# A Mamba and LSTM kernel: sigmoids made on ScalarE, and the LSTM's cell in plain VectorE operations

## The reference

```
def step(carry, xt):
    h, c = carry
    g = xt @ wih.T + h @ whh.T + bih + bhh
    i, f, gg, o = jnp.split(g, 4, axis=-1)
    c = jax.nn.sigmoid(f) * c + jax.nn.sigmoid(i) * jnp.tanh(gg)
    h = jax.nn.sigmoid(o) * jnp.tanh(c)
    return ((h, c), h)
...
comb = jnp.concatenate([m, lf, lb], axis=-1)
return comb @ fusion_w.T + fusion_b
```

## Time and profile before

| | |
|---|---|
| median of 3 runs | 2211.43 us (2204.95 to 2212.78) |
| span of the profiled execution, first to last instruction | 2159.5 us |
| median less that span | 51.9 us |
| VectorE busy in the span | 1645.7 us |
| ScalarE busy | 1298.3 us |
| GpSimd busy | 1011.2 us |
| TensorE busy | 1857.5 us |

### The profile page before, as it was taken

The page is one execution under the profiler, slowest core; times in us unless marked ns, Lnnn a source line. Parts: engine busy times, 40 slices in busy tenths (PEclk is TensorE's granted clock), DMA queues, the critical chain, the costliest instruction groups (busy, mean ns, idle before and its releaser), DMA issues. The chain is left out here.

```text
span 2159.5 us, 49411 instructions
## 1 busy us (share of the span) xinstructions
PE 1857.5 (86%) x19547; PEld 1357.8 (63%) x19547; DVE 1645.7 (76%) x2609; ACT 1298.3 (60%) x2660; POOL 1011.2 (47%) x775
## 2 busy tenths in 40 slices
PE   7888888889888867897878878889788699999999
PEld 4444444444443323444568877767676599999999
DVE  4999999999999996678465442346554589999897
ACT  5777777777776645114345444252456388888886
POOL 1777777777777773110017777300440033333333
PEclk9999999999999999899679999898899699999999
DMA  3544444444444442520038889501730411112000
GB/s 130 167 132 132 126 137 132 132 132 127 128 139 140 132 137 55 126 45 1 7 100 236 258 257 256 139 1 73 231 114 12 187 64 64 65 65 69 14 7 7
DMA packets 98037, 241.63 MB, mean 112 GB/s; under 512 B 15024, under 2 KB 48320, under 8 KB 95504
## 3 DMA queue, kind: packets, MB, share of 16 engines
q1 hardware_dynamic: 89120, 218.12, 32.7%
q0 software_dynamic: 7680, 15.74, 3.2%
q10 hardware_dynamic: 1008, 4.62, 0.6%
HBM read 226.25 MB, written 12.19 MB: 110 GB/s over the span
## 5 line engine op out<-in xcount | busy, mean ns | idle before, releaser
L1119 POOL TENSOR_TENSOR dBu<-du,Bs 128x858 f32<-128x858 f32 (+1 forms) x240 | 588.2, 2452 | 203.4 <-DVE hst L1046 94.6
L574 PE MATMUL py<-hst,ident 128*128 128x429 f32 (+1 forms) x960 | 416.7, 565 | 95.9 <-DVE hst L1056 95.1
L1046 DVE TENSOR_TENSOR_SCAN hst<-dA,dBu 128x858 f32<-128x858 f32 (+1 forms) x240 | 457.8, 1908 | 17.1 <-ACT dA L889 13.7
L889 ACT ACTIVATE dA<-dt,negA 128x416 f32<-128x416 f32 (+1 forms) x480 | 269.5, 596 | 177.2 <-DVE hst L1046 175.6
L574 PEld LDWEIGHTS py<-hst,ident 128*128 128x128 f32 x960 | 183.6, 202 | 292.3 <-DVE hst L1056 169.0
L3444 POOL TENSOR_TENSOR hm<-h,mw 128x264 f32<-128x264 f32 x128 | 89.7, 701 | 391.0 <-DVE h L3424 391.0
L1056 DVE TENSOR_TENSOR hst<-hst,Cs 128x858 f32<-128x858 f32 (+1 forms) x240 | 246.5, 1027 | 0.0
L3315 PE MATMUL pg<-hs,wh 128*128 128x66 f16 x6144 | 218.8, 194 | 4.8 <-issue 4.7
L3315 PE MATMUL pg<-xm,wi 128*128 128x66 f16 x6144 | 214.6, 195 | 6.8 <-issue 5.4
L3315 PEld LDWEIGHTS pg<-hs,wh 128*128 128x128 f16 x6144 | 204.8, 98 | 8.6 <-issue 5.1
L3315 PEld LDWEIGHTS pg<-xm,wi 128*128 128x128 f16 x6144 | 202.0, 98 | 11.3 <-issue 5.9
(11 more groups left out here) (568 smaller groups left out, 3458.8 us busy)
## 6 DMA issues: line engine op xcount, KB each, us to landing
wb<-sf_w SPq DMA_DIRECT2D x96, 514.0 KB, 4.9
Bs<-bc_rows SPq DMA_DIRECT2D x96, 429.0 KB, 4.6
Cs<-bc_rows SPq DMA_DIRECT2D x96, 429.0 KB, 3.5
mw<-route_weights SPq DMA_DIRECT2D x8, 2112.0 KB, 10.1
wb<-gf_w SPq DMA_DIRECT2D x24, 514.0 KB, 4.9
Bs<-bc_rows SPq DMA_DIRECT2D x24, 396.0 KB, 5.0
Cs<-bc_rows SPq DMA_DIRECT2D x24, 396.0 KB, 4.6
mb<-route_masks SPq DMA_DIRECT2D x8, 1088.0 KB, 5.8
```

Of the source, the lines that this page charges most:

```text
L574: return nc.tensor.matmul(out, weight, moving, **kw)
L889: last = a(o, by_seq(dt[:, j % 2, h, 0:n])[:, :, 1:S], ACT.Exp, scale=negA[:, l, h * DST + k:h * DST + k + 1])
L1046: v.tensor_tensor_scan(hst[:, g % HR, 0:2 * n], dA[:, g % 2, 0:2 * n], dBu[:, g % 2, 0:2 * n], 0.0, ALU.mult, ALU.add).then_inc(h_ready, 1)
L1119: g_.tensor_tensor(dBu[:, g % 2, 0:2 * n].rearrange("p (a n) -> p a n", a=2), du[:, j % 2, :, 0:n], Bs[:, q % NBS, k % BG, 0:n].unsqueeze( ...
```

## The change

Each step gets one more activation: after the four tanhs ScalarE turns the three tanhs of half gates into sigmoids in place, (x/2 + 1/2) over 3 x 64 columns, with the column of halves `half` that GpSimd sets once. It waits on `tanhed` for the third tanh. The cell is then the plain one. tanh(g) and the cell lie side by side in `gc`, so that both products are one multiply over 2 x 64 columns (`prod`), and an add makes the cell. h is one multiply. Nothing is doubled, and the two halvings of weights go.

```
-        cz = sb("cz", [128, 2, NB])
-        ig = sb("ig", [128, NB])
+        half = sb("half", [128, 1])
+        gc = sb("gc", [128, 2, NB])
+        prod = sb("prod", [128, 2, NB])
...
             def lstm(t):
                 if t == 0:
                     pe.wait_ge(l_loaded, 112)
-                    pe.wait_ge(lw_ready, 3)
                     pe.wait_ge(z_gated, 2)
...
                 for g in range(3):
-                    a(act3[:, g, :], pre[:, g, :], ACT.Tanh, scale=0.5, bias=lb[:, 2, g:g + 1])
-                a(cz[:, 0, :], pre[:, 3, :], ACT.Tanh, bias=lb[:, 0, 3:4]).then_inc(gated, 1)
+                    last = a(act3[:, g, :], pre[:, g, :], ACT.Tanh, scale=0.5, bias=lb[:, 2, g:g + 1])
+                last.then_inc(tanhed, 1)
+                a(gc[:, 0, :], pre[:, 3, :], ACT.Tanh, bias=lb[:, 0, 3:4])
+                act.wait_ge(tanhed, t + 1)
+                a(act3, act3, ACT.Identity, scale=0.5, bias=half[:, :]).then_inc(gated, 1)
 
             def lstm_cell(t):
                 act.wait_ge(c_ready, t + 1)
-                a(tc[:, :], cz[:, 1, :], ACT.Tanh, scale=0.5).then_inc(tc_ready, 1)
+                a(tc[:, :], gc[:, 1, :], ACT.Tanh).then_inc(tc_ready, 1)
...
-            a(whh[:, :, :, :], whh[:, :, :, :], ACT.Copy, scale=0.5).then_inc(lw_ready, 1)
-            a(fw[:, 1, :], fw[:, 1, :], ACT.Copy, scale=0.5).then_inc(lw_ready, 1)
...
             def lstm_c(t):
                 dve.wait_ge(gated, t + 1)
                 if t >= 1:
+                    dve.wait_ge(c_ready, t)
+                v.tensor_tensor(prod[:, :, :], act3[:, 0:2, :], gc[:, :, :], ALU.mult).then_inc(prods_ready, 1)
+                dve.wait_ge(prods_ready, t + 1)
+                if t >= 1:
                     dve.wait_ge(tc_ready, t)
-                    dve.wait_ge(c_ready, t)
-                v.scalar_tensor_tensor(out=ig[:, :], in0=act3[:, 0, :], scalar=1.0, in1=cz[:, 0, :],
-                                       op0=ALU.add, op1=ALU.mult).then_inc(prods_ready, 1)
-                v.scalar_tensor_tensor(out=act3[:, 1, :], in0=act3[:, 1, :], scalar=1.0, in1=cz[:, 1, :],
-                                       op0=ALU.add, op1=ALU.mult).then_inc(prods_ready, 1)
-                dve.wait_ge(prods_ready, 2 * t + 2)
-                v.scalar_tensor_tensor(out=cz[:, 1, :], in0=act3[:, 1, :], scalar=0.5, in1=ig[:, :],
-                                       op0=ALU.mult, op1=ALU.add).then_inc(c_ready, 1)
+                v.tensor_tensor(gc[:, 1, :], prod[:, 0, :], prod[:, 1, :], ALU.add).then_inc(c_ready, 1)
...
-                v.scalar_tensor_tensor(out=hr[:, t % 2, :], in0=act3[:, 2, :], scalar=1.0, in1=tc[:, :],
-                                       op0=ALU.add, op1=ALU.mult).then_inc(r_ready, 1)
+                v.tensor_tensor(hr[:, t % 2, :], act3[:, 2, :], tc[:, :], ALU.mult).then_inc(r_ready, 1)
```

More of the change, by code:

```diff
@@ L499, in mamba_lstm @@
             stage(nc, "wop_ready wop_kept cent_ready cent_kept sq_ready var_ready var_kept var_logged rstd_ready m_scaled m_done"))
-        (diag_ready, bias_set, lw_ready, gates_ready, gated, prods_ready, c_ready, tc_ready, r_ready, hs_kept, fused, fused_added) = ctx.enter_context(
-            stage(nc, "diag_ready bias_set lw_ready gates_ready gated prods_ready c_ready tc_ready r_ready hs_kept fused fused_added"))
+        (diag_ready, bias_set, lw_ready, gates_ready, half_set, tanhed, gated, prods_ready, c_ready, tc_ready, r_ready, hs_kept, fused, fused_added) = ctx.enter_context(
+            stage(nc, "diag_ready bias_set lw_ready gates_ready half_set tanhed gated prods_ready c_ready tc_ready r_ready hs_kept fused fused_added"))
         b_loaded = ctx.enter_context(stage(nc, " ".join(f"b_loaded{k}" for k in range(NBS))))
@@ L920, in _ @@
             decay(2)
-            act.wait_ge(lw_ready, 3)
+            act.wait_ge(lw_ready, 1)
+            act.wait_ge(half_set, 1)
             lstm_gates(0)
@@ L977, in _ @@
             v.memset(dA[:, :, :], 0.0).then_inc(dA_zeroed, 1)
-            v.memset(cz[:, 1, :], 0.0)
+            v.memset(gc[:, 1, :], 0.0)
             def soften(j):
@@ L1099, in _ @@
             g_.memset(edge[:, 1:2], 4000.0 / 32).then_inc(edge_set, 1)
+            g_.memset(half[:, :], 0.5).then_inc(half_set, 1)
             g_.memset(whh[:, :, :, :], 0.0).then_inc(l_zeroed, 1)
```

## The result

The changed kernel takes 2246.63 us (2244.49 to 2252.69, 5 runs) against 2211.43 (2204.95 to 2221.88) before: 1.0156 times, 95% interval 1.0135 to 1.0177. It is slower by some 35 us, where -0.15 had been forecast, and lies outside the range of 2204 to 2219.

A forecast was written before the change was run, and what follows sets the result against it. VectorE was taken to set the pace, except in ScalarE's chain to scan 8. Losses of 1.46 us from ScalarE's added work minus 1.61 us saved on VectorE gave -0.15 us, so 2211.3 us, range 2204 to 2219.

The forecast's parts named there:

- the cell on VectorE: LSTM cell's operations on VectorE: product to scan 0.465 us after the change, 0.07 less; add of 228 ns.
- The operation for h: VectorE's multiply that makes h in each LSTM step: would still take 0.13 us of VectorE.
- the saving of 0.07 us a step: VectorE's cell: 0.07 us less per step, arriving in 23 of the 33 steps, 1.61 us.
- ScalarE's activation: Added operation over 192 columns in PSUM: 378 ns long, ScalarE held 0.29 us longer per step.
- The 303 ns that the prediction set aside: Trainium skill's formula for the added 192-column ScalarE operation; with it the sum would be near -0.8 us.
- its delay is mostly swallowed: ScalarE's later gates: mostly absorbed by idle and existing waits, leaving 1.46 us of losses in all.
- Dropping the halvings: Two ScalarE activations before the scans go: worth 0, at most 0.9 us if dt were not the limit.
- B: Rival: ScalarE's added operation is exposed in every step, 9.6 us slower, 2221.0 us; chance 0.07.
- B2: Rival: exposed in every step, no overlap and a real wait on the tanh, 14.9 us, 2226.3; chance 0.03.
- A: Rival: VectorE's durations add up and ScalarE's work stays hidden, 4.5 us faster, 2206.9 us; chance 0.10.
- VectorE sets the pace: LSTM stretch from 50 to 623 us: VectorE is busy 555.0 of 573.0 us, ScalarE has slack on average.
- ScalarE's idle for the cell: Sign: ScalarE's idle while waiting for the cell state falls from 8.5 us to about 4.

The follow-up runs named there:

- b_again: The kernel before, unchanged, run once more for a second profile: a run of 2217.83 us with a span of 2215.9 us.
- a_pool_memset: The changed kernel with GpSimd's multiply dBu left out and zeros written over the same columns instead; timed once, 2214.87 us.
- experiment 4: The kernel before with only an added ScalarE identity activation over 3x64 columns, gates released after it: 2218.77 us, ratio 1.0008.
- a_split: The changed kernel with the two products apart, i*g into SBUF and f*c in place in PSUM: 2217.62 us, ratio 1.0005.

## Why the prediction was wrong

**The step that failed** is the cell on VectorE: "That the add is a plain multiply-or-add of 64 columns changes nothing: such an operation lasts 228 ns where the fused one lasts 224". Its price came from the row of L1658, which has both inputs in SBUF too, but is from a stage in which GpSimd only issues indirect DMAs (L2683, L2688). The prediction compared kinds and shapes of operations and not where their inputs lie and what GpSimd does meanwhile. The change took the PSUM input away from the cell's last operation by merging the two products into an SBUF tile. What the runs showed in its place: the add lasts 1259 ns in the mean, because it waits for the GpSimd multiply that is running. That is 34 us over the 33 steps, of a loss of some 35.

The sum against `b_again`, from the first scan of item 0 to that of item 11 (timelines, added up over the 33 steps): 593.7 us before, 627.4 after, +33.7. Product to what follows the cell: 17.7 us before, 49.5 after, +31.9. VectorE's waits for gates: 3.0 and 7.5, +4.5. Its waits before scans (in the whole stage): 18.9 and 16.6, -2.3. Together +34.1, against the 33.7 measured.

**It was in sight.** GpSimd mostly starts its multiply when a scan ends, as VectorE starts the product by C, which reads two SBUF tiles as well. In the trace of before, VectorE's

```profile
379.94 1.55 DVE L1056 TENSOR_TENSOR hst<-hst,Cs 128x858 f32<-128x858 f32 x1
```

lasts 0.52 us longer than the usual 1.03, and GpSimd had just begun

```profile
379.87 0.72 POOL L1096 TENSOR_TENSOR wt<-w,cw 128x256 f32<-128x256 f32 x1
```

which ends at 380.59. The group's mean of 1027 ns hid it. Of the 240 products by C 13 last 1.17 to 1.56 us, each with a GpSimd multiply that had begun before it. The usual case is the other way round: the product by C begins first, GpSimd's multiply waits inside its own recorded 2.6 us, and does its work from the product's end on, just when the cell comes. (The one at 424.04 us after the change, with no product by C in its way, lasts 1.80 us.)

The scan shows the other side. It reads its decay `dA` from PSUM, so it has one SBUF input. In item 6 of before it starts at 388.10, inside

```profile
386.50 2.66 POOL L1119 TENSOR_TENSOR dBu<-du,Bs 128x858 f32<-128x858 f32 x1
```

and takes its usual 1.93 us. Of the 240 scans of before 217 start inside a GpSimd multiply that has at least 0.3 us to go, and none lasts longer than 1.947 us. This is also why the blocked time is lost: before the change the next scan ran beside the rest of GpSimd's multiply, and now the add stands in front of it and waits for that rest.

The Trainium skill (SBUF — State Buffer, Who interferes with whom) says that a VectorE instruction with two SBUF inputs contends with a GpSimd instruction that reads SBUF, not with one that only writes it. The same page of the Trainium skill (SBUF: two separate sides) says that whichever starts first has the shared ports for its whole instruction. The runs agree on all three points: 1259 against 225 ns, 225 ns inside GpSimd's zeroing, and half the loss back with half the instruction. The prediction did not weigh this rule.

**Rightly priced.** Without GpSimd's reads, in `a_pool_memset`, product to scan takes 0.319 + 0.143 = 0.46 us by the timeline, against 0.465 forecast; in the changed kernel's own two unblocked steps, 3 and 12, it is 0.47. The operation for h is unchanged at 0.13. So the saving of 0.07 us a step is real, and buried. ScalarE's activation takes 405 ns, not 378, and starts 0.20 us after the fourth tanh, as forecast. From its start to that of the next instruction it is 0.304 us, so that ScalarE is held 0.30 us, against 0.29 forecast. (The 303 ns that the prediction set aside as too low for the duration is close to this distance.) That its delay is mostly swallowed is borne out by experiment 4 as far as its interval goes, and by the waits for gates in `a_split`, 2.9 us against 3.0 in `b_again`. Dropping the halvings was not tried apart; the changed kernel's first scan starts at 46.7 us, before it 46.3 and 47.4, so nothing shows.

**Of the rivals**, B and B2 lay on the right side, B2 nearest (2226.3, still 20 us short), and both by the wrong mechanism: ScalarE's added work costs nothing that can be told. Neither was a wait inside a VectorE instruction, and the prediction had no rival for that. A fell with the sign of the change. The lack of idle on VectorE, read as "VectorE sets the pace", was read rightly, which is why the blocked 1.03 us a step went nearly whole into the time. Of the listed signs, ScalarE's idle for the cell was to fall to about 4 us and rose to 35.0, which alone would have told of a late cell.

## What to carry to other kernels

When an edit merges, moves or retypes a VectorE operation, write down for each one which inputs lie in SBUF and which in PSUM, before and after, and what GpSimd does at that moment. Take prices only from rows where both match; one input in PSUM made this add 0.22 us where it had mostly been 1.55. A duration that spreads widely over one shape (look at min, median and max of the line, not its mean) can be a wait that no waits view lists; lay the two engines' timelines side by side.

## What the runs showed of the hardware

- A VectorE operation with two SBUF inputs that comes while GpSimd's multiply runs costs what is left of that multiply, whatever its own size: one column took 1469 ns in the mean with two SBUF inputs and 152 ns with one.
- One with an input in PSUM does not wait: the 217 scans that start inside a GpSimd multiply last 1.947 us at most, where 1.934 is the median.
- GpSimd's zeroing, which only writes, doesn't block the add: 225 ns wholly inside a zeroing of 1.80 us.
- A GpSimd instruction queued behind the running one doesn't overtake the waiting add: with the multiply in halves, the add went in between the halves in 28 of the 33 steps.
- Neither engine's wait shows as idle time: it is part of the recorded duration, 1.56 us for this add and 2.58 us for a multiply that takes 1.80 unhindered.
